# Another order of stages at both ends of a macaron block, and a margin for the scan in its order model

## What is computed

```python
x = x + 0.5 * ffn(layernorm(x))      # ternary weights, inner width 1408
x = x + mamba(layernorm(x))
x = x + 0.5 * ffn(layernorm(x))      # the same weights

# ffn:   hdn = silu((x @ gate_w.T) * gate_s) * ((x @ up_w.T) * up_s);  (hdn @ down_w.T) * down_s
# mamba: h, gate = split(x @ W_in.T)                   # 1024 channels each
#        h = silu(causal_conv4(h) + conv_b)
#        ts, B, C = split(h @ Wx.T, [128, 16, 16]);  each RMS-normed with its weight
#        delta = softplus(ts @ Wdt.T + dt_bias)
#        for each step t:  s = exp(delta_t * A) * s + delta_t * B_t * h_t;  y_t = sum_n(s * C_t)
#        (y + D * h) * silu(gate) @ Wout.T
```

## Time and profile before

| | before |
|---|---|
| median of 3 runs | 2962.04 us (2957.05 to 2974.04) |
| profiled execution: its own time | 2956.89 us |
| its span, first to last instruction | 2955.0 us |
| mean granted TensorE clock | 0.892 |
| busy: TensorE, DVE, POOL, ACT | 2435.7, 2494.6, 2259.7, 1760.2 us |

### The profile page before, as it was taken

The page is one execution under the profiler, slowest core; times in us unless marked ns, Lnnn a source line. Parts: engine busy times, 40 slices in busy tenths (PEclk is TensorE's granted clock), DMA queues, the critical chain, the costliest instruction groups (busy, mean ns, idle before and its releaser), DMA issues. The chain is left out here.

```text
span 2955.0 us, 37471 instructions
## 1 busy us (share of the span) xinstructions
PE 2435.7 (82%) x12266; PEld 1989.5 (67%) x12266; DVE 2494.6 (84%) x3131; ACT 1760.2 (60%) x2995; POOL 2259.7 (76%) x1370
## 2 busy tenths in 40 slices
PE   7677876877778899888988799788997796698888
PEld 5465665766656677667766688667776684576767
DVE  5649997888898898899988998799978898799963
ACT  5446566575756557565667667566566566654621
POOL 2247868896896679978898789978898689988842
PEclk9878897977889899998999999898998896798899
DMA  7634562674487456874578556874478654657464
GB/s 278 251 108 133 180 238 72 200 248 137 129 280 276 147 176 218 305 273 154 160 262 297 182 179 207 302 276 159 153 236 278 214 189 168 223 170 248 146 225 137
DMA packets 293945, 606.60 MB, mean 205 GB/s; under 512 B 23024, under 2 KB 23792, under 8 KB 293744
## 3 DMA queue, kind: packets, MB, share of 16 engines
q1 hardware_dynamic: 293744, 604.13, 60.9%
HBM read 451.47 MB, written 152.57 MB: 204 GB/s over the span
## 5 line engine op out<-in xcount | busy, mean ns | idle before, releaser
L1140 POOL TENSOR_TENSOR sbuf<-dus,bring 128x1024 f32<-128x1024 f32 x512 | 1220.8, 2400 | 268.5 <-PE pt L1180 173.0
L520 PE MATMUL pm<-xT,wring 128*128 128x512 f32 x4352 | 1128.8, 408 | 81.3 <-DVE hd L782 27.3
L520 PEld LDWEIGHTS pm<-xT,wring 128*128 128x128 f32 x4352 | 818.0, 194 | 256.3 <-issue 59.4
L1154 ACT ACTIVATE pa<-dls,cst 128x512 f32<-128x512 f32 x1024 | 691.6, 688 | 460.9 <-DVE sbuf L1163 450.3
L1180 PE MATMUL pt<-ident,sbuf 128*128 128x128 f32 x4096 | 666.9, 301 | 236.0 <-DVE sbuf L1163 103.7
L1180 PEld LDWEIGHTS pt<-ident,sbuf 128*128 128x128 f32 x4096 | 534.2, 155 | 375.8 <-DVE sbuf L1163 140.8
L1163 DVE TENSOR_TENSOR_SCAN sbuf<-pa,carry,sbuf 128x512 f32<-128x512 f32 x512 | 637.4, 1274 | 74.7 <-POOL sbuf L1140 39.0
L1163 DVE TENSOR_TENSOR_SCAN sbuf<-pa,sbuf 128x512 f32<-128x512 f32 x512 | 610.8, 1213 | 74.2 <-ACT pa L1154 60.0
L595 PE MATMUL pm<-wring,act 128*128 128x512 f32 x2176 | 590.0, 415 | 54.0 <-DVE hd L1067 22.1
L1191 DVE SCALAR_TENSOR_TENSOR acc<-pt,cT,acc 128x512 f32<-128x512 f32 x768 | 550.9, 742 | 61.9 <-PE pt L1180 55.1
L595 PEld LDWEIGHTS pm<-wring,act 128*128 128x128 f32 x2176 | 408.9, 196 | 150.9 <-DVE hd L1067 25.4
(11 more groups left out here) (136 smaller groups left out, 2144.3 us busy)
## 6 DMA issues: line engine op xcount, KB each, us to landing
wring<-wsp SPq DMA_DIRECT2D x408, 512.0 KB, 4.4
bring<-b_d SPq DMA_DIRECT2D x256, 256.0 KB, 3.9
xn_d<-tb SPq DMA_DIRECT2D x24, 1024.0 KB, 9.4
xnb<-xn_d SPq DMA_DIRECT2D x19, 1024.0 KB, 7.3
x_d<-tb SPq DMA_DIRECT2D x16, 1024.0 KB, 6.5
u_d<-hd SPq DMA_DIRECT2D x64, 256.0 KB, 4.3
sg_d<-hd SPq DMA_DIRECT2D x64, 256.0 KB, 4.0
tb<-x_d SPq DMA_DIRECT2D x16, 1024.0 KB, 7.1
```

Of the source, the lines that this page charges most:

```text
L520: f = lambda e, pw=pw, px=px, k=k, first=(i == 1), end=(i == total): e.matmul(pm[b][:, 0:n], lhs(pw, k), rhs(px, k), start=first, stop=end)
L1140: t_p = S.op("pool", lambda e, s2=s2, s3=s3, h=h: e.tensor_tensor(sbuf[:, s3, h * m:(h + 1) * m, :], dus[:, h * m:(h + 1) * m, :], bring[: ...
L1154: t_e = S.op("act", lambda e, k=k, i=i, pb=pb, n=n: e.activation(pa[pb][:, :], dls[:, k, :], ACT.Exp, scale=col(C_A + i * N + n)), dl_tok[ ...
```

## The change

There are three edits. `SLACK_S` goes from 0 to 0.3 (in the model's us), `SLACK_TP` from 0.5 to 0.4. A list `CLOSING` is taken out of the rounds and put at the end. And quarters can be placed inside an `ffn1` at two points, after its second and its sixth column pair, with an `OPENING` that makes use of it.

```diff
-SLACK_S = 0.0
-SLACK_TP = 0.5
+SLACK_S = 0.3
+SLACK_TP = 0.4
...
-INSIDE = (("ffn1", "dt1"),)
...
-OPENING = (... ("ffn1", 1), ("prep_in", 1), ("dt0", 1), ("dt1", 1), ("ffn1", 2), ("dt2", 1), ("dt3", 1), ("prep_in", 2), ("dt0", 2), ("dt1", 2))
+OPENING = (... ("ffn1", 1), ("prep_in", 1), ("ffn1", 2), ("dt0", 1), ("dt1", 1), ("dt2", 1), ("dt3", 1), ("prep_in", 2), ("ffn1", 3), ("dt0", 2), ("dt1", 2))
+CLOSING = (("dt1", 7), ("post", 5), ("dt2", 7), ("post", 6), ("dt3", 7), ("ffn2", 5), ("ffn2", 6), ("post", 7), ("ffn2", 7))
...
-                    if j == J // 2 and within:
-                        within()
+                    if within and j in within:
+                        within[j]()
...
-            order = [x for x in order if x not in OPENING]
+            order = [x for x in order if x not in OPENING and x not in CLOSING]
+            order += CLOSING
...
-            for a, b in zip(order, order[1:]):
-                if (a[0], b[0]) in INSIDE:
-                    inner[a] = b
+            for a, b, n in zip(order, order[1:], order[2:]):
+                if a[0] == "ffn1" and b[0] == "dt0":
+                    inner[a] = {1: b, 5: n}
+                elif a[0] == "ffn1" and b[0] == "dt1":
+                    inner[a] = {5: b}
```

More of the change, by code:

```diff
@@ L45 @@
 CUT = 2
-OPENING = (("ffn1", 0), ("prep_in", 0), ("dt0", 0), ("dt1", 0), ("gates", 0), ("dt2", 0), ("dt3", 0), ("ffn1", 1), ("prep_in", 1), ("dt0", 1), ("dt1", 1), ("ffn1", 2), ("dt2", 1), ("dt3", 1), ("prep_in", 2), ("dt0", 2), ("dt1", 2))
+OPENING = (("ffn1", 0), ("prep_in", 0), ("dt0", 0), ("dt1", 0), ("gates", 0), ("dt2", 0), ("dt3", 0), ("ffn1", 1), ("prep_in", 1), ("ffn1", 2), ("dt0", 1), ("dt1", 1), ("dt2", 1), ("dt3", 1), ("prep_in", 2), ("ffn1", 3), ("dt0", 2), ("dt1", 2))
+CLOSING = (("dt1", 7), ("post", 5), ("dt2", 7), ("post", 6), ("dt3", 7), ("ffn2", 5), ("ffn2", 6), ("post", 7), ("ffn2", 7))
 ROUND = (("ffn1",0),("dt1",1),("dt2",1),("post",LAG),("dt3",1),("prep_in",0),("ffn2",LAG),("dt0",0))
@@ L1282, in build @@
             inner = {}
-            for a, b in zip(order, order[1:]):
-                if (a[0], b[0]) in INSIDE:
-                    inner[a] = b
+            for a, b, n in zip(order, order[1:], order[2:]):
[3 more added lines that the diff above has]
+                    inner[a] = {5: b}
             for kind, c in order:
-                if (kind, c) in inner.values():
+                if any((kind, c) in x.values() for x in inner.values()):
                     continue
@@ L1301, in build @@
                     following[0] = KIND[later[0][0]], later[0][1]
-                more = [lambda k=k, n=n: stage[k](n) for k, n in [inner.get((kind, c))] if k] if (kind, c) in inner else []
+                more = [{j: (lambda k=k, n=n: stage[k](n)) for j, (k, n) in inner[kind, c].items()}] if (kind, c) in inner else []
                 stage[kind](c, *more)
```

## The result

The changed kernel takes 2946.41 us (median of 5 runs, 2940.03 to 2948.28); the kernel before, run beside it, 2962.04 (2954.19 to 2974.04, 5 runs). The ratio is 0.9932, with a 95% interval of 0.9908 to 0.9955: 20 us (13 to 27) or 0.7% faster. The forecast was 2932, the range 2897 to 2970. The direction and the range were right; the size was two thirds of the forecast. (The two medians lie 15.6 us apart, a ratio of 0.9947 and about half of the forecast, so the size is known only roughly.) By the median, the result lies between the forecast and the rival in which the idle time only moves (2952), and nearer to that rival.

What follows compares the result with a forecast made beforehand. No engine was full; VectorE (DVE) was busiest, and only its 460.4 us of idle time could change. Tail -9.7, opening -12.0 and closing -8 make -29.7: 2956.9 to 2927.2, with 5.15 to the median 2932 us, range 2897 to 2970.

Steps and rivals of the forecast that it cites:

- the idle time only moves: Rival: M's waits vanish but DVE idles at post(6) and the last four groups; only the tail stays, 2952; chance 0.20.
- Tail, -9.7: Kernel's end: 48 matmuls move ahead of the last four scan groups, so acc's transposes follow the last addition; bounds 0, -9.7.
- Closing, -8: Last chunks: one post between each two quarters instead of three quarters in a row before post(5); -8, bounds 0 and -15.7.
- Opening, -12.0: Chunks 1 and 2: first two quarters move into the next FFN, cutting DVE idle time by 6.9 and 5.1; bounds 0, -20.5.
- as the mixed row is what the place becomes: Opening: the moved quarters' DVE work would idle at the middle scans' ratio, 0.117 us per busy us.
- The exposure that I costed at nothing: Chunk 1: after its first two scans, scan 1 may wait for the second quarter; margin 16 us, taken as 0.
- a hole of the size that I had named as a sign against me: Sign of a wrong forecast: a hole of more than 10 us before the third scan of chunk 1.
- 5.5 scan groups lie between: Chunk 1, from L985 to the third scan: 5.5 groups at 10.8 us, 59 us, enough to cover the 43 needed.
- Margin, 0 within 15 us: All 1024 scans: SLACK_S and SLACK_TP save or add a tenth of 148.9 us idle time, +-15; taken as 0.
- Both rivals on it: Margin does more: 2882 or 2902, chance 0.12; margin holds ready scans back: 3009, chance 0.08.
- Half clock, nothing: Rival: throttled transposes of 13 scan-only groups set the pace, +25 us, 2957, chance 0.05; the forecast took no cost.
- DVE's 2494.6 us stay: Whole kernel: same instructions, so DVE's busy time stays at 2494.6 us and only its 460.4 us of idle time can change.

Runs made afterwards that it cites:

- kernel with separated quarters: Kernel before with only the quarters of chunk 7 separated by posts and FFNs, ffn2(5) still ahead of post(6); 2968.46 us, ratio 0.9989.
- two half closings: On the kernel before, either the quarters of chunk 7 separated (0.9989) or post(6) put ahead of ffn2(5), quarters still in a row (0.995).
- twelve runs: The twelve follow-up kernels, in three groups, each group on one chip with the kernel before; ratios to it from 0.9919 to 1.0044.

## Why the prediction was right, and where not

**Tail, -9.7.** Locally right: the gap is 0.05 us and the stretch behind the last addition 10.0 us shorter. As a term of the sum it was too simple. The kernel with separated quarters and the opening alone cover the tail as well, at 0.9989 and 1.0005: the stretch from dt0(7) to the last addition took 4.4 and 37.4 us more there than before (in the opening alone with 4.75 scan groups more). The 48 matmuls that leave the tail have to be reached earlier; whether that itself delays the last addition is not shown.

**Closing, -8.** With the tail -17.7, measured -16 (-20 to -12): about the right size, but not for the reason given. I put the gain down to the quarters that no longer stand in a row, and treated post(6)'s new place as the price. The two half closings show the reverse (0.9989 and 0.995). "M waits one cycle (28 us) rather than two before post(5)" came true: with separated quarters M waits 23.7 us there, where it was 26.0 and 25.1, and 91.7 in all places where it was 113.3 (26.0, 25.1 and 35.0 between 2461.3 and 2592.3, and 27.2). The step that failed is to price that as idle time of DVE: from dt0(7) to the last addition it was 37.7 us, where it was 34.2. Why post(6) ahead of ffn2(5) pays stays open; only its effect is measured.

**Opening, -12.0.** In the opening alone the idle time in its own stretch fell by 11.5 us, as forecast, but not the total (1.0005). In the changed kernel, with the margins, not even that is left: 101.0 us are idle up to the x-projection of chunk 3 (757.5 less 656.5; 96.9 in the closing alone), with 67.25 groups done. The step that failed is "as the mixed row is what the place becomes": it took the stretch as if it stood alone. M that gets ahead leaves scan groups undone, 4 of them, and these are done at the end, where idle time rose by 7.6 us (34.2 to 41.8). So for this part the rival "the idle time only moves" was right. The exposure that I costed at nothing was there. Windows from the end of the second scan of chunk 1 to the start of the third, before, in the changed kernel and in the opening alone:

```profile
533.70:548.90 15.20, 14.02 (x62) 11.27 (x61) 5.78 (x10) 5.47 (x10) 6.86 (x6) 1.00 0.85 303
549.00:566.30 17.30, 13.11 (x60) 10.55 (x58) 7.24 (x16) 7.45 (x9) 8.09 (x7) 0.96 0.87 312
539.20:555.30 16.10, 15.75 (x69) 12.40 (x68) 0.02 (x1) 1.38 (x2) 4.86 (x3) 1.00 0.87 294
```

DVE is idle for 9.4 us there before, for 10.1 in the changed kernel (7.8 of them in one piece) and for 16.1 in the opening alone, in one piece: a hole of the size that I had named as a sign against me. The step that failed is "5.5 scan groups lie between", which fits the count over TensorE's list (32.5 less 27), where the transposes come behind the scans. In the changed kernel DVE had 14 scan instructions, 3.5 groups, left from the L985 at 513.74 to the third scan at 566.26, and the quarter took 52.5 us and not 43.

**Margin, 0 within 15 us.** Alone +13, on top of the closing +21, on top of the opening -10, with both other parts between 0 and -7: beyond the bounds in one case, inside them in the others, and not one number. Both rivals on it describe a half. The margin does step around the scans' waits (108.2 us in the changed kernel, 148.4 in the same one with the old margins). But the work that steps ahead delays others. The margins alone show it in the page's fifth part:

```profile
L1163 DVE TENSOR_TENSOR_SCAN sbuf<-pa,sbuf 128x512 f32<-128x512 f32 x512 | 610.4, 1212 | 87.3 <-ACT pa L1154 60.5
L1163 DVE TENSOR_TENSOR_SCAN sbuf<-pa,carry,sbuf 128x512 f32<-128x512 f32 x512 | 636.5, 1270 | 50.6 <-ACT pa L1154 29.2
...
L1191 DVE SCALAR_TENSOR_TENSOR acc<-pt,cT,acc 128x512 f32<-128x512 f32 x768 | 549.0, 740 | 86.3 <-PE pt L1180 80.0
```

The scans wait 11.0 us less than in the kernel before (137.9 for 148.9), the additions 24.4 more (86.3 for 61.9).

**Half clock, nothing.** While post(6) waits, the granted clock is 0.56, near the lower of the two levels, with TensorE busy for 37.2 us of 77.2, and DVE is idle for 9.4 of 77.2 us: 12%, more than the tenth that I had named as a sign against me. But the releasers do not point to the transposes. Groups by line of that stretch of the changed kernel (busy us, mean ns, idle before and releasers):

```profile
L1163 DVE TENSOR_TENSOR_SCAN sbuf<-pa,sbuf 128x512 f32<-128x512 f32 x28 | 33.1, 1209 | 5.2 <-ACT pa L1154 5.2
L1191 DVE SCALAR_TENSOR_TENSOR acc<-pt,cT,acc 128x512 f32<-128x512 f32 x26 | 18.5, 738 | 3.2 <-POOL acc L1198 1.7 <-PE pt L1180 1.2
L1163 DVE TENSOR_TENSOR_SCAN sbuf<-pa,carry,sbuf 128x512 f32<-128x512 f32 x11 | 13.4, 1268 | 1.0 <-ACT pa L1154 1.0
```

Only 1.2 us are put down to transposes on TensorE; 6.2 are waits for the exponentials on ACT. No run set the clock apart from the order, so a cost by way of other waits is not excluded. The rule of the Trainium skill ("TensorE: Matmul & The Clock Gate", Part 1), that the array is throttled unless activity releases it, agrees with the clock of this hole; that the time followed it is not seen here.

**The frame.** "DVE's 2494.6 us stay" was off: 2503.6 after the change, and between 2494.8 and 2508.2 in the twelve runs. The instructions did not get longer: the durations of DVE's 3131 instructions add up to 2723.3 us before and to 2716.6 after the change. But neighbours overlap by 228.7 us in the one trace and by 213.0 in the other, and DVE's work is broken by 462 and by 495 idle spells. The 15.7 us of overlap that went, less the 6.7 by which the durations fell, are the 9.0. Half of the 18.1 us of idle time that left DVE came back this way.

**The sum.** Forecast: -9.7 - 12.0 - 8 + 0 = -29.7. Measured: -16 for the closing with the tail, about 0 for the opening, and -5 to -7 for the margins on top (0.9948 to 0.9932 and 0.9925, within the intervals and not seen in the medians): -20 to -22, and by the medians -16 and -19. One of three sized terms was worth nothing and another came out for a reason that was not the one given, so that the total fell into its range owes something to luck.

## What to carry to other kernels

When one thread is sped up at one end of a pipelined kernel, count what the other thread has done by the same mark: 31.5 us that buy four groups fewer are no gain until it is shown what these groups cost where they end up. A wait that is taken away is worth what the total says, so cost the place to which the work moves, as well as the one that it leaves. A scheduler's margin and a hand-written order are to be tried in combination: here the same margins ran at 1.0044 with one order and, with the other, at 0.9971 where that order alone had 1.0005.

## What was not expected

From the x-projection of chunk 3 to dt0(7), four kernels (the one before, the closing alone and its two halves) run the same stages with 140.5 scan groups and have as many instructions on DVE, ACT and POOL (1619, 1607, 738). That stretch took 1457.6, 1474.8, 1470.7 and 1465.8 us in their profiled executions, a spread of 17.2 us. DVE was busy for 1300.29, 1301.66, 1300.08 and 1299.86 us in them, so nearly all of the spread is waiting, and the granted clock was 0.94, 0.93, 0.93 and 0.93. Two single traces of this kernel can't tell a change of 10 us apart. The stretch in which it must show may do better: from dt0(7) to the last addition, two executions of the changed kernel took 418.8 and 419.7 us.
